# One-hots in pairs of columns, and matmuls of constants on TensorE, in a one-core graph network and mixture-of-experts kernel

## The reference

```python
xn = layernorm(x)
h = xn @ W;  deg = segment_sum(1, dst);  dinv = where(deg > 0, rsqrt(max(deg, 1)), 0)
x = x + segment_sum(h[src] * (dinv[src] * dinv[dst])[:, None], dst) + linear_attention_0(xn)
g = layernorm(x) @ gate_w + gate_b             # 16 experts, the best two of each node
x = x + layernorm(xg + sum_k softmax(top2)_k * expert_k(xg)) * gamma + beta   # xg = layernorm(x)
xn = layernorm(x);  agg = zeros.at[dst].set(xn[src])
x = x + concat(xn, agg) @ W1.T + b + transformer_layer_with_linear_attention(xn)
w = layernorm(x) @ wr + br;  the 3124 nodes of greatest w:
x = layernorm(x) + (gelu(layernorm(x)[sel] @ w1 + b1) @ w2 + b2) * w[sel]  added at those nodes, + x
```

## Time and profile before

| | us |
|---|---|
| median of the runs | 2835.33 (2834.97 to 2849.89, 3 runs) |
| the profiled execution | 2826.39 |
| its span, first to last instruction | 2824.6 |

### The profile page before, as it was taken

How to read it: one execution, slowest core, us unless ns; L and a number is a source line. 1 busy time by engine, 2 the same in 40 slices (tenths; PEclk the granted TensorE clock), 3 DMA queues, 4 the chain that set the end, 5 groups by cost and what they waited for, 6 DMA issues and landing times. The chain is left out here.

```text
span 2824.6 us, 48636 instructions
## 1 busy us (share of the span) xinstructions
PE 2284.8 (81%) x12908; PEld 1934.7 (68%) x12909; DVE 1469.6 (52%) x4060; ACT 871.2 (31%) x2530; POOL 1610.1 (57%) x2188
## 2 busy tenths in 40 slices
PE   7966677677676766555959999979999999994798
PEld 6744555555454554344859999968878999993798
DVE  8734444343444444445762223258876888886311
ACT  2521222221111111112723333346653433441233
POOL 4746666666666667674026555468866555550233
PEclk9977688788788777667579999989999999997899
DMA  4043333332333333332313334332221111111122
GB/s 153 26 133 88 88 87 88 90 87 84 90 91 88 89 89 93 91 91 69 126 58 117 104 120 136 104 89 89 80 68 51 45 45 43 43 43 55 27 36 31
DMA packets 138715, 227.60 MB, mean 81 GB/s; under 512 B 26683, under 2 KB 99088, under 8 KB 138642
## 3 DMA queue, kind: packets, MB, share of 16 engines
q0 software_dynamic: 56336, 142.96, 18.3%
q1 hardware_dynamic: 81186, 82.10, 8.8%
q10 hardware_dynamic: 1120, 1.71, 0.2%
HBM read 175.36 MB, written 51.30 MB: 80 GB/s over the span
## 5 line engine op out<-in xcount | busy, mean ns | idle before, releaser
L902 POOL DMA_INDIRECT all_XN<-h_table,l_srcI x784 | 777.2, 991 | 403.8 <-issue 246.8
L1102 PE MATMUL gcn_acc<-all_XN 128*128 128x256 f32 x768 | 249.9, 474 | 117.0 <-DVE all_X L995 72.9
L1102 PE MATMUL gcn_acc<-all_XN,gcn_hot 128*128 128x256 f32 x800 | 250.0, 461 | 80.2 <-DVE all_X L995 38.6
L1102 PEld LDWEIGHTS gcn_acc<-all_XN 128*128 128x128 f32 x768 | 174.2, 237 | 173.6 <-DVE all_X L995 77.1
L1102 PEld LDWEIGHTS gcn_acc<-all_XN,gcn_hot 128*128 128x128 f32 x800 | 176.3, 230 | 137.2 <-issue 64.8
L836 ACT COPY gcn_seen_sb<-gcn_seen 128x392 f32<-128x392 f32 x98 | 47.5, 485 | 581.4 <-remote 459.9
L1778 ACT ACTIVATE moe_hidden<-moe_hid_ps,moe_b 128x128 f32<-128x128 f32 x420 | 131.6, 364 | 287.2 <-PE moe_hid_ps L1858 271.4
L995 DVE SCALAR_TENSOR_TENSOR all_X<-gcn_acc,all_XN,all_X 128x256 f32 x392 | 170.8, 477 | 81.0 <-remote 60.1
L1858 PEld LDWEIGHTS moe_hid_ps<-moe_xst,held_held 128*128 128x128 f32 x1680 | 204.2, 193 | 11.9 <-issue 7.3
L1858 PE MATMUL moe_hid_ps<-moe_xst,held_held 128*128 128x128 f32 x1680 | 207.5, 277 | 1.8 <-DVE moe_xst L1799 1.7
L1865 PE MATMUL moe_y_ps<-held_held,moe_hidden 128*128 128x256 f32 x840 | 198.9, 380 | 0.5 <-ACT moe_hidden L1778 0.5
(11 more groups left out here) (405 smaller groups left out, 4849.3 us busy)
## 6 DMA issues: line engine op xcount, KB each, us to landing
held_held<-in_e_w SPq DMA_DIRECT2D x32, 512.0 KB
slots_out<-moe_y SPq DMA_DIRECT2D x105, 128.0 KB
all_XN<-h_table,l_srcI POOLq DMA_INDIRECT x784
all_X<-in_x SPq DMA_DIRECT2D x7, 896.0 KB, 11.1
rows_table<-all_XN SPq DMA_DIRECT2D x7, 896.0 KB, 4.1
z_table<-held_held SPq DMA_DIRECT2D x49, 128.0 KB
x_table<-all_XN SPq DMA_DIRECT2D x49, 128.0 KB, 1.7
out<-all_X SPq DMA_DIRECT2D x49, 128.0 KB, 1.7
```

What stands on the lines that cost most here:

```text
L902: nc.gpsimd.indirect_dma_start(msg[b][:, c, :], None, self.h_table, bass.IndirectOffsetOnAxis(self.srcI[:, GE * g + c:GE * g + c + 1], 0)) ...
L1102: last = nc.tensor.matmul(acc[b % NA][:, :], hot[b % NH][:, c, :], msg[b][:, c, :], start=(c == 0), stop=(c == GE - 1))
```

## The change

Six parts. (1) Front: lo has 64 values and hi 98, and both one-hots are laid out [edge pair, value, 2], so that the innermost row is a pair of edge columns. The count comes out as 64 x 98 and is brought into 128 x 49 by a copy and two matmuls with a shifted identity; the clamp of the count moves behind two tiles' norms; dst's lane for the gather is computed later. (2) Gather: the register load moves ahead of the last groups on DVE and PE, and POOL loads it without its wait. (3) Gate: one matmul of 512 constant columns a tile, 8 ahead of the loop and 24 ahead of the lists; ACT's `number` goes; the list's one-hots are written by one DVE op per chunk, in pairs, multiplied by the partition's number by ACT (chunks 0, 2, 4) or DVE (1, 3, 5, 6); the marks become stationary and the one-hots move, so the list comes out in the wanted layout without the transpose. (4) `busy` with 16, 40 and 14 constant matmuls ahead of the first tiles of experts, combine and select. (5) Attend: the last tile's output base on DVE. (6) Select: the lists' one-hots in pairs, 5 chunks of 10 tiles, the product by the partition's number on ACT.

```diff
-            iota_16 = piece(P * HE // 2).bitcast(BF16).rearrange("p (n c) -> p n c", c=HE)
+            iota_2 = piece(P).bitcast(BF16).rearrange("p (n k) -> p n k", k=2)
...
+                    def in_pairs(cols, t, n):
+                        return cols[:, ds(HE * t, HE)].rearrange("p (c k) -> p c k", k=2).unsqueeze(2).broadcast_to([P, HE // 2, n, 2])
                     def low(t, p):
                         after(dve, hot_used, t - 1)
-                        nc.vector.tensor_tensor(lo_hot[p][:, :, :], dst_lo[:, ds(HE * t, HE)].unsqueeze(1).broadcast_to([P, P, HE]),
-                                                iota_16[:, :, :], ALU.is_equal).then_inc(hot_ready, 1)
+                        nc.vector.tensor_tensor(lo_hot[p][:, :, :, :], in_pairs(dst_lo, t, LOW), iota_2[:, 0:LOW, :].unsqueeze(1).broadcast_to([P, HE // 2, LOW, 2]), ALU.is_equal).then_inc(hot_ready, 1)
...
                     dve.wait_ge(hot_used, T)
-                    nc.vector.tensor_scalar(deg1[:, :], deg[:, :], 1.0, None, ALU.max).then_inc(deg_chain, 1)
+                    nc.vector.tensor_copy(halves[:, :, :], by_half.rearrange("p (t k) -> p k t", k=2)).then_inc(halves_ready, 1)
                     for k in range(2):
                         norms(k, k, 0)
+                    dve.wait_ge(deg_done, 1)
+                    nc.vector.tensor_scalar(deg1[:, :], deg[:, :], 1.0, None, ALU.max).then_inc(deg_chain, 1)
...
-                            last = nc.tensor.matmul(deg[:, :], lo_hot[p][:, :, c], hi_hot[p][:, :, c],
+                            last = nc.tensor.matmul(by_half, lo_hot[p][:, c // 2, :, c % 2], hi_hot[p][:, c // 2, :, c % 2],
...
                     project(0, 0)
+                    pe.wait_ge(halves_ready, 1)
+                    pe.wait_ge(spread_ready, 2)
+                    nc.tensor.matmul(deg[:, :], spread_low[:, LOW:3 * LOW], halves[:, 0, :], start=True, stop=False)
+                    nc.tensor.matmul(deg[:, :], spread_low[:, 0:2 * LOW], halves[:, 1, :], start=False, stop=True).then_inc(deg_done, 1)
                     project(1, 1)
...
+    def busy(self, bank, count):
+        ones = self.ones[:, :].bitcast(BF16)
+        for _ in range(count):
+            self.nc.tensor.matmul(bank[:, :].rearrange("p (k n) -> p k n", k=2), ones[:, 0:P], ones.unsqueeze(1).broadcast_to([P, 2, 2 * P]), start=True, stop=True)
...
-                        if c >= 4:
-                            number(c - 4)
...
+                    for c in by_act:
+                        h = high[c % HB][:, :, :, :, :].rearrange("p i k n u -> p i k (n u)")
+                        act.wait_ge(high_ready, c + 1)
+                        nc.scalar.activation(h[:, :, 1, :], h[:, :, 0, :], ACT.Copy, scale=self.place_no).then_inc(high_by_act, 1)
...
-                        for i in range(PC):
-                            last = nc.vector.tensor_scalar(high[c % HB][:, i, :], iota_b[:, 0:MAX_TILES], tile_of[:, c, i:i + 1], float(CT * c + i % CT + 1), ALU.is_equal, ALU.mult)
-                        last.then_inc(high_ready, 1)
+                        pairs = [P, PC // 2, MAX_TILES, 2]
+                        nc.vector.tensor_tensor(high[c % HB][:, :, 0, :, :], tile_of[:, c, :].rearrange("p (i u) -> p i u", u=2).unsqueeze(2).broadcast_to(pairs),
+                                                iota_2[:, :, :].unsqueeze(1).broadcast_to(pairs), ALU.is_equal).then_inc(high_ready, 1)
+                        if c in by_dve:
+                            h = high[c % HB][:, :, :, :, :].rearrange("p i k n u -> p i k (n u)")
+                            dve.wait_ge(high_ready, c + 1)
+                            nc.vector.tensor_scalar(h[:, :, 1, :], h[:, :, 0, :], self.place_no, None, ALU.mult).then_inc(high_by_dve, 1)
...
+                        self.busy(list_bank, 1)
...
+                    self.busy(list_bank, 8)
                     pe.wait_ge(consts_in, 48)
...
                     nc.tensor.matmul(column_ps[:, 0:E], ones[:, :], taken[:, C, CT, :], start=True, stop=True).then_inc(counted, 1)
+                    self.busy(list_bank, 24)
...
-                            last = nc.tensor.matmul(list_ps[0:MAX_TILES, :, :], high[c % HB][:, i, :], tables[:, c, i, :, :],
+                            last = nc.tensor.matmul(list_ps, tables[:, c, i, :], high[c % HB][:, i // 2, :, :, i % 2],
...
+                    self.busy(y_bank, 16)
...
+                    self.busy(z_bank, 40)
...
-                    for c in range(0, T, XC):
+                    for c in range(0, TP, XC):
...
-                        nc.vector.tensor_tensor(lane_hot[:, ts, :], place_b[:, 0, ts].unsqueeze(2).broadcast_to([P, XC, P]),
-                                                iota_bf[:, :].unsqueeze(1).broadcast_to([P, XC, P]), ALU.is_equal)
+                        nc.vector.tensor_tensor(lane_hot[:, cs, :, :], in_pairs(place_b[:, 0, ts], P), to_all(P), ALU.is_equal)
...
+                    self.busy(total, 14)
```

More of the change, by code:

```diff
@@ L355, in front_stage @@
         GP = G // 2
+        LOW = P // 2
+        HIGH = ROWS // LOW
         assert ET == HE * T and NX % 2 == 0 and T % 2 == 1
@@ L360, in front_stage @@
             part = s.sb("part", [P, ET], I32)
-            dst_lo = self.dst_lo
+            dst_lo = s.sb("dst_lo", [P, ET], BF16)
             dst_hi = s.sb("dst_hi", [P, ET], BF16)
+            warm = s.sb("warm", [P, 1])
+            halves = s.sb("halves", [LOW, 2, T])
+            spread_low = s.sb("spread_low", [LOW, 3 * LOW])
             dst_rows = s.sb("dst_rows", [GP, 2 * GE * P], I32)
@@ L912, in gather @@
                                                          bass.IndirectOffsetOnAxis(wide_idx[:, c:c + 1], 0)).then_inc(wide_in, 16)
-                    pool.wait_ge(summed, G)
-                    wide_groups(pool, gather)
+                    wide_groups(pool, gather, wide_count(pool))
                 @block.vector
@@ L1235, in gate @@
         HB = 4
-        assert C * CT == T and 2 * C * P * PC <= 2 * KB * ROWS
+        marks, tile_words = C * PC * P // 2, PC * MAX_TILES
+        assert C * CT == T and marks + (HB - 1) * tile_words <= KB * ROWS and PC % 2 == 0
         with ExitStack() as ctx:
@@ L1265, in gate @@
             iota_b = s.sb("iota_b", [P, P], BF16)
[L1266 to L1269 removed]
+            iota_2 = s.sb("iota_2", [P, MAX_TILES, 2], BF16)
+            flat = self.XT[:, :, :].rearrange("p b n -> p (b n)")
+            tables = flat[:, 0:marks].bitcast(BF16).rearrange("p (c i n) -> p c i n", c=C, i=PC)
+            places = [flat[:, marks + i * tile_words:marks + (i + 1) * tile_words] for i in range(HB - 1)] + [self.held[1][:, 0:tile_words]]
+            high = [w.bitcast(BF16).rearrange("p (i k n u) -> p i k n u", i=PC // 2, k=2, u=2) for w in places]
+            start_each = self.held[1][:, 0:T * E].bitcast(BF16).rearrange("p (a b) -> p a b", b=E)
             start_b = s.sb("start_b", [P, E], BF16)
[L1271 removed]
+            tile_of = s.sb("tile_of", [P, C, PC], BF16)
             zero = s.sb("zero", [P, E])
@@ L1330, in copy_xxt @@
                         nc.scalar.copy(xxt[t % 2][:, :, :], turned[t % 2][:, :, :]).then_inc(xxt_ready, 1)
-                    def number(c):
-                        act.wait_ge(mark_ready, CT * c + CT)
-                        nc.scalar.activation(tables[:, c, :, 1, :], tables[:, c, :, 0, :], ACT.Copy, scale=self.place_no).then_inc(table_ready, 1)
                     for c in range(C):
@@ L2287, in output_base @@
                     def output_base(t, p, h):
+                        if isinstance(t, int) and t == T - 1:
+                            return
                         after(pool, x4_ready, t + 1)
@@ L2551, in _ @@
                 def _(act):
+                    for c in range(0, TP, XC):
+                        cs = slice(c // 2, (c + XC) // 2)
+                        act.wait_ge(chain, LISTED + c // XC + 1)
+                        nc.scalar.activation(node_part[:, cs, 0, :, :], tile_hot[:, cs, :, :], ACT.Copy, scale=self.place_no).then_inc(place_ready, 1)
                     act.wait_ge(w_in, 80)
@@ L2611, in _ @@
                     nc.vector.tensor_copy(iota_bf[:, :], iota[:, :])
+                    nc.vector.tensor_copy(iota_2[:, :, :], iota[:, :].unsqueeze(2).broadcast_to([P, P, 2]))
+                    nc.vector.memset(place_b[:, :, T:TP], -1.0)
                     dve.wait_ge(ranked, 1)
```

135 lines of the change are left out of this document (77 added, 58 removed).

## The result

| | us |
|---|---|
| before, first series (7 runs) | median 2841.91 (2834.97 to 2849.89) |
| changed kernel, first series (7 runs) | median 2825.66 (2814.37 to 2835.12) |
| ratio, 95% interval | 0.9939 [0.9915, 0.9964] |
| its profiled execution | 2835.12, span 2833.4 |

Later series on other chips gave the ratio 0.9908 [0.989, 0.9925] and 0.9922 [0.9904, 0.994]. The kernel is faster by 16 to 25 us; I had forecast 36. The profiled execution of the changed kernel happens to be the longest of its seven, and the one of before (2826.39) is shorter than any of its seven runs, so the two spans compare the wrong way round (+8.8 us). The stages show where that lies.

A forecast was written before the change was run, and what follows sets the result against it. Stages run one after another, each with its own bound; POOL's gathers pace the gather. Terms sum to 36 us, taking the profiled 2826.39 to about 2790 and the median of 2835.33 to 2799, range 2784 to 2822.

The forecast's parts named there:

- front: Stage before the gather: smaller pair ops, cheaper matmuls and a smaller iota cast gain 9.3 us (bounds 2 and 17).
- turn, register load: Gather to gate: moving the register load ahead of the last groups gains 0.7 us (0 to 1.0).
- gate's loop: Gate's tiles: at full clock a tile costs about 0.85 us instead of 1.18; gain 9.5 us (bounds 3 and 13).
- lists and gate's end: Behind the gate's loop: one compare per chunk gains 5.6 us, dropping PE's transpose and one op 0.65.
- experts, combine first tiles: First matmuls of both stages: constants ahead raise the clock, gaining 0.8 us in experts and 1.3 in combine.
- select's first tile: Select's first 32 matmuls: constants ahead raise the clock, gaining 2.2 us (0 to 2.6).
- last output base: End of attend: moving the last tile's output base from POOL to DVE gains 0.1 us.
- so I take the clock as full after a warm-up: Gate's loop: a 512-column matmul between each tile's transposes, and 8 ahead, give full clock; about 0.85 us a tile.
- Rival (a): Gate's clock stays at 0.50: tile 1.6 us, chunk 12.2, loop 17 us longer, total 2829; chance 0.10.
- The phase alone: Front's first 13 tiles, DVE working alone: about 1.49 us a tile for 1.80; gain counted as 4.5 us.
- the phase beside: Front's next 36 tiles, counts beside norms: 2.13 us a tile for 2.30, gain 6 us (bounds 0 and 14).
- the tail: End of the front's beside phase: copying the degrees and two fp32 matmuls before the clamp cost 1.2 us net.

The follow-up runs named there:

- pool_wait: Changed kernel with POOL's wait for the last sums back ahead of its register load: turn to the gate 3.09 us against 0.59, gate's loop 78.9 us.

## Why the prediction was wrong

The sum, term by term, with what the profiles show:

| term | forecast | measured |
|---|---|---|
| front | -9.3 | -15.8 to -16.8 |
| turn, register load | -0.7 | -2.1 to -2.5 |
| gate's loop | -9.5 | **+12.4** |
| lists and gate's end | -6.25 | -5.9 |
| experts, combine first tiles | -2.1 | 0 (stages +0.5 to +2.4) |
| select's first tile | -2.2 | -1.3 to -2.6 |
| select's lists | -6.1 | -6.2 |
| last output base | -0.1 | -2.6 to -3.5 |

**The step that failed** is "so I take the clock as full after a warm-up". I had argued by likeness: the front has the same transposes, with real matmuls between them, and a clock of 1.00. One matmul a tile did not lift the clock in two profiles of this kernel and for 3.4 us in the third; three a tile did, after 4 us in one kernel and 15 in another. Rival (a) is what happened, in kind: PE at 98% busy had not lifted the clock before, and the row said so. I gave it 0.10. Its price was near too: 1.6 us a tile against 1.52 measured, 12.2 a chunk against 11.54, 17 us more for the loop against 12.4. The Trainium skill ("TensorE: Matmul & The Clock Gate", Part 4) has transposes not counted as busy, and no run here speaks against that; that one other matmul a tile would be enough was my own step.

The price at full clock was right, the room that the one matmul takes included: 0.80 us a tile for my 0.85, chunks of 6.9, 6.9 and 7.2 for my 7.4. In `pool_wait`, at full clock, the fifth chunk begins 35.2 us into the gate, in the kernels without constants at 41.9, and from there these need 37.2 to the loop's end. Put together, an estimate from these rows, a clock that stays up would give a loop of 72.4 us, 9.3 less than before; I had forecast 9.5. No kernel here got there: the clock didn't last to the late chunks with one a tile, and three a tile, which held it, take so much room that the loop is as long as at half clock without them (79.9 and 79.1 us). From the fourth chunk on DVE bounds at 9.5 us at either clock, so it is only in three chunks that the clock can gain. The gain from ACT's removed `number` is real, 1.3 us in each of two late chunks: without constants they take 9.5 instead of 10.8.

**The front** gained for another reason than mine, and more. The phase alone gave 5.3 us (forecast 4.5), the phase beside 12.4 (6), and the tail cost 1.9 (1.2). I put PE's 0.109 us a matmul down to loading 128 columns of weights and took 0.09 for 64. The cost was the moving operand's step of 32 bytes. With PE out of the way, and POOL's ops at a mean of 0.50 us for 0.65, the beside phase came to the bound that I had given as the most possible, DVE's own 1.90 (1.88), and not to 2.13. That the forecast missed by no more is in part luck: the front's 6.5 to 7.5 us too much hide a third of what the gate lost against it.

**Turns.** I gave the last output base 0.1 without a reason (the op takes 0.96 us on POOL, 0.42 on DVE). What counts is which engine ends the stage: two experiments, at two turns, give 2.5 and 4.1 us for POOL as the last.

**First tiles.** As feared in the text, PE is idle again between the constants and the data; in experts and combine the clock was 0.50 for the first matmuls. Combine is 2 us longer in all changed kernels, also in the one without constants, at 0.1 us for two tiles. POOL's op for the reciprocal root there (`comb_ln_b_rs`, 49 times) takes 675 to 685 ns on average against 644 and 645. The cause of both stays open.

With the failed term at +12.4 in place of -9.5 and the others as forecast, the sum would have been 14 us; with all measured terms it is some 20, and the three series show 16, 25 and 22.

## What to carry to other kernels

Before adding idle matmuls to lift TensorE's clock, ask of each stretch what bounds it at full clock and subtract the room that they take there; don't count on one that held the clock in one kernel to hold it in the next; test with none, one and several, and read the granted clock, since a likeness to another stage proved nothing. Lay out one-hots so that both DVE's innermost row and the step with which PE reads them are small: the pair layout kept DVE's rate and took PE's matmuls of that shape from 196 to 57 ns. And look at which engine ends a stage: give the last small op to one that is not POOL.

## What the runs showed of the hardware

- A bfloat16 compare with rows of two elements (both inputs repeated or stepped) runs as fast as one with rows of 16: 0.95 us for 1568 elements either way, 0.68 and 0.69 for 1024, and 0.82 us for 1280 in select, where single values spread over a row took 1.09 us for 896.
- A bfloat16 moving operand at a step of 32 bytes took 2.0 ns a column (98 columns, 196 ns) at a clock of 1.00, with the stationary operand at the same step; at 4 bytes, 98 columns took 57 ns.
- The granted clock in the gate's loop with one added matmul of 512 columns a tile was 0.50 throughout in four profiles, up for less than a chunk in two, and 1.00 for one and a half to four chunks in three (8, 16 and 24 ahead). In the 4 us before it fell from 1.00 in these three, PE was busy for 3.52 (16 ahead), 2.02 (8) and 2.98 (24).
- A stage that POOL left last let DVE begin the next one 3.09 and 4.93 us after its own last op; with POOL done earlier it was 0.59 and 0.87.
- The gather took 1009 to 1017 us in three of the series and 1139 to 1172 in the other two, with most issues of an indirect DMA at 0.95 us on POOL in all.
